# First mixture of experts on sorted 256-token tiles inside the attention batches

## What is computed

```
x  = x + tanh(g_xattn[0]) * attention0(layernorm(x), ctx)        # "att0": 16 heads of 8, 512 keys
x  = x + tanh(g_ffn[0])   * top1_mixture(layernorm(x))           # "m0": 8 experts, 128 -> 512 -> 128
x  = x + tanh(g_xattn[1]) * block(layernorm(x), ctx)             # "att1" self (256 keys), "att2" cross (512), "f" MLP
x  = x + tanh(g_ffn[1])   * layer(layernorm(x))                  # "att3" causal, "m1" 4 experts, top 2

def top1_mixture(x):                                             # x: 2048 tokens
    logits = x @ gate_w.T + gate_b
    top1 = argmax(logits, axis=-1)
    for e in range(8):
        h = relu(x @ w1[e].T + b1[e])
        y = h @ w2[e].T + b2[e]
        out = out + where(top1 == e, y, 0)
```

## Time and profile before

| | us |
|---|---|
| median of 3 runs | 1461.47 |
| lowest, highest | 1455.52, 1464.43 |
| the profiled execution | 1462.72 |
| its span, first to last instruction | 1460.9 |
| PE busy | 1272.8 |
| DVE busy | 861.5 |
| ACT busy | 692.7 |
| POOL busy | 306.1 |

### The profile page before, as it was taken

How to read it: one execution, slowest core, us unless ns; L and a number is a source line. 1 busy time by engine, 2 the same in 40 slices (tenths; PEclk the granted TensorE clock), 3 DMA queues, 4 the chain that set the end, 5 groups by cost and what they waited for, 6 DMA issues and landing times.

```text
span 1460.9 us, 25048 instructions
## 1 busy us (share of the span) xinstructions
PE 1272.8 (87%) x8296; PEld 664.8 (46%) x8296; DVE 861.5 (59%) x1890; ACT 692.7 (47%) x1064; POOL 306.1 (21%) x896
## 2 busy tenths in 40 slices
PE   3999899979999998788879998888888778879998
PEld 1444444534444443445434544444555556534333
DVE  2777767834443444577667776868665756533333
ACT  1466656633333432566646674554534334423333
POOL 3223222100001000233322231323232323100000
PEclk9999989989999999699979998998989879879999
DMA  7554544210001300455554453443324434220010
GB/s 187 162 154 143 147 128 131 74 48 8 15 22 38 104 3 22 131 165 167 156 177 128 145 148 102 133 124 111 106 78 131 120 99 138 63 55 21 22 29 15
DMA packets 163174, 144.32 MB, mean 99 GB/s; under 512 B 11739, under 2 KB 136931, under 8 KB 163043
## 3 DMA queue, kind: packets, MB, share of 16 engines
q1 hardware_dynamic: 163046, 142.72, 33.8%
HBM read 78.98 MB, written 62.91 MB: 97 GB/s over the span
## 4 chain that ended last, share of the span: by engine, by line
issue 65%; POOLq 22%; PE 10%; DVE 1%; DMA 1%; ACT 0%; DVEq 0%; POOL 0%; SPq 0%; PEldq 0%; ACTq 0%
POOLq L871 5%; POOLq L844 4%; PE e_ps L1580 3%; PE av_ps L1591 3%; PE e_ps L1581 3%; POOLq L841 2%; POOLq L846 2%; POOLq L879 2%; POOLq L881 2%; POOLq L883 2%; PE misc L1572 1%; POOLq L859 1%; POOLq L890 1%; POOLq L898 0%; PE misc L1360 0%
## 5 line engine op out<-in xcount | busy, mean ns | idle before, releaser
L930 ACT ACTIVATE prob<-e_ps 128x1024 f32<-128x1024 f32 (+1 forms) x384 | 378.2, 988 | 245.4 <-PE e_ps L1411 176.1
L1094 DVE TENSOR_REDUCE nmax<-s_ps 128x1 f32<-128x512 f32 x512 | 332.8, 685 | 116.3 <-PE s_ps L1374 114.1
L1411 PE MATMUL e_ps<-Qst,Kst 75*128 75x256 bf16 x1408 | 245.4, 288 | 19.4 <-DMA Qst<-mrow 12.1
L1374 PE MATMUL s_ps<-Kst,Qst 72*128 72x512 bf16 x512 | 208.9, 412 | 39.4 <-DVE nmax L1094 29.0
L1429 PE MATMUL av_ps<-prob,Vx 128*32 128x256 f32 (+1 forms) x3072 | 223.8, 411 | 0.8 <-ACT OT L935 0.8
L1411 PEld LDWEIGHTS e_ps<-Qst,Kst 75*128 75x128 bf16 x1408 | 139.8, 103 | 90.3 <-issue 24.4
L1218 DVE TENSOR_TENSOR prob<-prob,s_ps 128x512 f32<-128x512 f32 x128 | 87.8, 686 | 147.7 <-ACT prob L980 147.0
L980 ACT ACTIVATE prob<-e_ps,b 128x512 f32<-128x512 f32 x128 | 87.9, 687 | 147.5 <-PE e_ps L1510 146.9
L1510 PE MATMUL e_ps<-FB,wbig 128*128 128x512 f32 x256 | 137.4, 628 | 0.0
L1517 PE MATMUL av_ps<-prob,wbig 128*128 128x512 f32 x256 | 128.1, 592 | 0.0
L1429 PEld LDWEIGHTS av_ps<-prob,Vx 128*32 128x32 f32 x3072 | 92.8, 116 | 72.3 <-issue 38.9
(11 more groups left out here) (178 smaller groups left out, 1684.5 us busy)
## 6 DMA issues: line engine op xcount, KB each, us to landing
q_parts<-qp SPq DMA_DIRECT2D x96, 192.0 KB, 2.4
k_parts<-kp SPq DMA_DIRECT2D x48, 384.0 KB, 3.4
Qst<-q_parts SPq DMA_DIRECT2D x128, 144.0 KB
Kst<-k_parts SPq DMA_DIRECT2D x64, 288.0 KB
k_parts<-kp SPq DMA_DIRECT2D x48, 192.0 KB, 2.4
Kst<-k_parts SPq DMA_DIRECT2D x64, 144.0 KB
ctxT<-in_ctxT SPq DMA_DIRECT2D x16, 256.0 KB, 4.8
wbig<-in_w SPq DMA_DIRECT2D x16, 256.0 KB, 4.9
```

Of the source, the lines that this page charges most:

```text
L930: act.activation(dst, src, ACT.Exp).then_inc(e_drained, 1)
L1094: ve.tensor_reduce(nmax[:, g, u, h % GH:h % GH + 1], s_ps[:, c % 2, :], AX.X, ALU.max, negate=True).then_inc(s_drained, 1)
L1374: last = pe.matmul(s_ps[:, c % 2, :], Qst[0:ROWS, par, s, u * P:u * P + P], Ks[0:ROWS, par, s, :], start=True, stop=True)
L1411: last = pe.matmul(o, Ks[0:KROWS, par, h, t * P:t * P + P], Qst[0:KROWS, par, h, :], start=True, stop=not a.rope)
```

## The change

RUNS is one run of 32 batches. `moe0_steps` is gone, and att1 follows att0 directly. The mixture is done for each half of the batches (0 to 3, 4 to 7):

- Per batch of att0, two batches later or for the last of a half right behind it: gate logits from `nT`, the choice for 2 tiles of 128 tokens, and `m0.rank`: five small bfloat16 matmuls with a triangular and a ones matrix that count, for each token, the tokens of the same expert before it. The normalized rows stay in SBUF (`zg`) instead of going to DRAM transposed.
- `m0.plan` (three DVE steps per half): tiles of 256 tokens per expert, at most 4 + 7 = 11; the expert of each tile (`widx`), and the row of each token in the sorted order (`ypos`).
- `m0.scatter`, 8 per half: POOL scatters 128 rows of 512 B each by `ypos` to `xs_rows` in DRAM, which two transfers at the start have filled with zeros. `m0.wload`, 11 per half: POOL gathers the expert's weights, 128 rows of 1156 numbers (4.6 KB, 592 KB in all), into a ring of 4.
- For each tile: `m0.xload` (128 KB, SP), `m0.xT` (2 transposes, ACT copies), `m0.h` (4 matmuls of 256 columns into one buffer of `e_ps`, four relus), `m0.down` (8 matmuls with the tokens as stationary operand, 128 columns, into `misc`; DVE adds the bias), a store to `ys_rows`.
- Tiles of the first half begin in batch 5 at its middle, one per slot; those of the second in batch 9 (att1) at its middle, two per slot. A tile's three steps are in three successive slots.
- For each batch of att1: `loadx` loads the residual rows and POOL gathers twice 128 rows of `ys_rows`; DVE gates and adds, takes statistics, normalizes (`xapply`); PE transposes (`xT`); SP stores both (`xstore`). att1's `loadin` is gone.
- POOL: instead of `drain`, each operation adds to a semaphore and the next waits for it; each step waits for its own kind's last result.
- `body`: `weave` spreads the steps that use `misc` evenly over the score and AV units of the slot.

Weights of the second mixture and the MLP are loaded from batch 11 on. `prob`'s ring no longer counts the mixture (`RING_AT`). Cut to its core:

```
-RUNS = [(0, B), (B, N)]
+RUNS = [(0, N)]
...
+        per, rate = tile_pace(g)          # 16 // slots of the attention the tiles lie in, for both
+        put(n, TILES_AT - 2, ("m0.xload", g, 0), ("m0.xload", g, 1))
+        for k in range(NT):
+            p = TILES_AT + k // rate * per
+            if k + WRING < NT:
+                put(n, p + 3 * per, ("m0.wload", g, k + WRING))
+            if k + 2 < NT:
+                put(n, p + per, ("m0.xload", g, k + 2))
+        p = TILES_AT + (NT - 1) // rate * per + 2 * per + 2
+        m = B + HALF * g
+        put(n, p, ("loadx", m, None))
+        put(n, p + 1, ("loadx", m + 1, None))
+        put(n, p + 2, ("xstat", m, None))
+        put(n, p + 4, ("xapply", m, None))
+        put(n, p + 5, ("xT", m, None), ("xstore", m, None))
+        put(n, p + 6, ("q", m, None), ("qsplit", m, None), ("xstat", m + 1, None))
+        put(n, p + 7, ("k", m, None), ("ksplit", m, 0))
+        put(n, p + 8, ("qstore", m, None))
+        put(n, p + 9, ("kstore", m, None))
...
+        for x in range((NT - 1) // rate + 3):
+            for lag, kind in ((2, "m0.down"), (1, "m0.h"), (0, "m0.xT")):
+                tiles = range(rate * (x - lag), rate * (x - lag) + rate)
+                steps += [(kind, g, k) for k in tiles if 0 <= k < NT]
...
+        units[1:1] = [[st] for st in tiles if st[0] == "m0.h"]
+        out.append(("E", n, s))
+        out += weave(units, chunks)
...
+                elif kind == "m0.wload":
+                    po.wait_ge(m0_planned, 2 * n + 1)
+                    if arg >= WRING:
+                        wait_drained(po, ("m0.down", n, arg - WRING))
+                    elif n:
+                        wait_drained(po, ("m0.down", n - 1, NT - 1))
+                    index = bass.IndirectOffsetOnAxis(ap=widx[:, n, arg:arg + 1], axis=0)
+                    po.indirect_dma_start(out=w_0[:, arg % WRING, :], out_offset=None, in_=dram["w_0"], in_offset=index) \
+                        .then_inc(m0_win[arg % WRING], 16)
+                elif kind == "loadx" and n >= B:
+                    par, g = n % 2, (n - B) // HALF
+                    po.wait_ge(m0_ystored[0], 16 * Y_EVEN * (g + 1))
+                    po.wait_ge(m0_ystored[1], 16 * Y_ODD * (g + 1))
+                    po.wait_ge(x_stats, n - 1)
...
+                elif kind == "m0.h":
+                    c = SLOT[st]
+                    pe.wait_ge(m0_win[arg % WRING], 16 * (w_uses(n, arg) + 1))
+                    wait_drained(pe, ("m0.xT", n, arg))
+                    pe.wait_ge(e_drained, c - 1)
+                    for t in range(H0 // P):
+                        last = pe.matmul(e_ps[:, c % 2, t * TILE:(t + 1) * TILE], w_0[:, arg % WRING, t * P:t * P + P],
+                                         xs_T[:, arg % 2, :], start=True, stop=True)
...
+            for g in range(B // HALF):
+                blank = dram["blank"].unsqueeze(0).to_broadcast([NT, TILE, D])
+                sp.dma_start(xs_rows[g].rearrange("(n r) d -> n r d", r=TILE), blank).then_inc(blank_stored, 16)
...
-                po.drain()
-                po.tensor_copy(parts[:, 1, c0:c1], r[:, c0:c1])
-                po.drain()
+                settled()
+                counted(po.tensor_copy(parts[:, 1, c0:c1], r[:, c0:c1]))
+                settled()
```

More of the change, by code:

```diff
@@ L33 @@
 E0, H0 = 8, 512
+HALF = B // 2
+GT = HALF * QT
+TILE = 256
+NT = HALF * SQ // TILE + E0 - 1
+WRING = 4
+WCOLS = 2 * H0 + H0 // P + D
 E1, H1 = 4, 384
@@ L170, in ffn_items, with tile_pace, moe0_items, put @@
     return it
+def tile_pace(g):
+    per = 16 // att(HALF * g + HALF + TILES_AT // 16).slots
+    return per, per
+def moe0_items():
+    it = {}
+    def put(n, p, *steps):
+        it.setdefault((n + p // 16, p % 16), []).extend(steps)
+    for b in range(B):
+        if b % HALF < HALF - 1:
+            for p, kind in ((3, "m0.gate"), (6, "m0.choose"), (9, "m0.rank")):
+                put(b + 2, p, (kind, b, None))
+    for g in range(B // HALF):
+        last = HALF * g + HALF - 1
+        n = last + 1
+        for p, kind in ((11, "m0.gate"), (12, "m0.choose"), (13, "m0.rank")):
+            put(n, p, (kind, last, None))
+        for k in range(3):
+            put(n, 14 + k, ("m0.plan", g, k))
+        for k in range(WRING):
+            put(n, 16 + k // 2, ("m0.wload", g, k))
+        for j in range(GT):
+            put(n, 17 + j // 2, ("m0.scatter", g, j))
+        per, rate = tile_pace(g)
[17 more added lines that the diff above has]
+        put(n, p + 9, ("kstore", m, None))
+    return it
@@ new lines, in tile_items @@
+def tile_items():
+    it = {}
+    for g in range(B // HALF):
+        per, rate = tile_pace(g)
+        n = HALF * g + HALF
+        for x in range((NT - 1) // rate + 3):
+            steps = []
+            for lag, kind in ((2, "m0.down"), (1, "m0.h"), (0, "m0.xT")):
+                tiles = range(rate * (x - lag), rate * (x - lag) + rate)
+                steps += [(kind, g, k) for k in tiles if 0 <= k < NT]
+            p = TILES_AT + x * per
+            it[(n + p // 16, p % 16 // per)] = steps
+    return it
@@ L173, with opens_half @@
+def opens_half(n):
+    return B <= n < 2 * B and n % HALF == 0
 FFN_ITEMS = ffn_items()
+TILES_AT = 24
+MOE0_ITEMS = moe0_items()
+TILE_ITEMS = tile_items()
 QUARTERS = 4
@@ L424, in ring_users, with out_count @@
     return user
+RING_AT = count(("E", "f.h", "m1.h"))
 USER = ring_users()
-IN_PER = {"att0": 16, "att1": 16, "att2": 32, "att3": 16}
+IN_PER = {"att0": 16, "att1": 0, "att2": 32, "att3": 16}
+OUT_PER = {"att0": 16, "att1": 32, "att2": 32, "att3": 32}
 def in_count(n):
     return sum(IN_PER[att(m).name] for m in range(n % 2, n + 1, 2))
+def out_count(n):
+    return sum(OUT_PER[att(m).name] for m in range(n % 2, n + 1, 2))
 def program(nc, dram, outs):
```

666 lines of the change are left out of this document (348 added, 318 removed).

## The result

| | before | changed |
|---|---|---|
| median (lowest to highest) of the runs side by side | 1462.95 us (1455.52 to 1473.35, 4) | 1400.11 us (1397.82 to 1415.43, 4) |
| ratio, 95% interval | 1 | 0.959 (0.950 to 0.968) |
| profiled execution, span | 1462.72, 1460.9 us | 1398.62, 1396.8 us |
| mean granted TensorE clock | 0.927 | 0.896 |

The account below looks back on a forecast made before the run. The first mixture's stage was taken as bound by PE columns, 7 of 8 for experts not chosen. Terms: -273 + 42 + 42 + 20 + 8 + 10 + 5 + 12 + 8 - 12 = -138, giving 1325 us, range 1264 to 1400.

Parts of the forecast that it names:

- What was removed: Between att0 and att1: the first mixture's own stage and the two seams around it go, 273 us less.
- tiles: On PE: 22 added tiles at 3.83 us each lengthen their slots by their whole price, 42 us per half.
- rival B: Tile slots bound by their chains, PE at 1.2 GHz in them, tiles cost double: 1395 us, chance 0.18.
- Late weights: Second half's tiles 4 to 10 in att1 meet weights just asked for: four slots of 5 us, 20 us (4 to 40).
- Start-up: Two blanking transfers on SP's queue ahead of batch 0's q and k parts delay the first exponential: 10 us (0 to 20).
- The way into att1: Loading, gathering, normalizing and transposing att1's inputs: 1.5 us for each of 8 batches, 12 us (0 to 15).
- POOL's semaphores: On POOL: semaphores in place of drains change nothing, 0 us (-5 to +5).
- the new order of bank steps: Spreading the misc bank's steps over each slot saves some 1 us per batch over 32 batches: -12 us (-35 to +15).
- 0.4 to 1 us each, hidden, 0 on the path: 54 weight loads, scatters and gathers issued by POOL: hidden by POOL's slack, adding 0 us to the path.
- Rival C: Each of 54 indirect transfers holds POOL and the maxima's chain for 4.45 us: 1545 us, slower, chance 0.05.
- the choice: Choosing, ranking and planning on DVE in att0, mostly hidden in idle time: 0.6 us a batch, 5 us (0 to 23).

Follow-up runs that it names:

- e6: Changed kernel without the weight reloads for tiles 4 to 10 of each half, which use weights already in the ring: 1381.7 us, ratio 0.943.
- e14: e13 with the old order of slot steps in att1 batches without a tile (8 and 11 to 15) too: 1380.0 us, ratio 0.944.
- e13: e9 with the choice of each half's last batch also in five steps over three places, plan and transfers one place later: 1366.9 us, ratio 0.932.
- e2: Changed kernel with the old order of slot steps in the batches of att2 and att3 alone: 1377.3 us, ratio 0.940.
- e3: Kernel before with only the new order of slot units and bank steps: 1494.5 us, ratio 1.021.
- e8: Changed kernel with 2 of the 8 scatters per half, all tiles still computed: 1391.2 us, ratio 0.948.
- e12: Changed kernel without the weight reloads for tiles 4 to 10 and with only two of eight scatters per half: 1366.3 us, ratio 0.931.
- e9: Changed kernel with old order in att2 and att3, choice in five pieces except each half's last batch, and blanking stores issued later: 1361.5 us, ratio 0.935.
- e5: Changed kernel with the choice of batches 0-2 and 4-6 in five pieces at five places instead of one block: 1391.5 us, ratio 0.948.
- e4: Changed kernel with POOL ordered by drains again instead of semaphores: 1425.1 us, ratio 0.975.

## Why the prediction was wrong, point by point

What was removed was right: the stage and both seams went. The **tiles** were right where nothing else interferes: from the third slot with a tile (272.9 us) ten slots follow that take 5.5 to 6.3 us, 5.95 on average from exponential to exponential, at a granted clock of 1.00. So a tile adds 5.95 - 2.14 = 3.8 us (forecast 3.83). That also fells rival B, though its 1395 us is near the time: its cause, tile slots at 1.2 GHz, isn't there in att0, and the loss lies in other places. Only batch 9, at 0.75, has something of it.

**Late weights**: forecast 20, measured 18 at most (e6), though with three direct waits of 10.3 us in all and not four of 5. **Start-up**: forecast 10, measured 7.0. By the Trainium skill, DMA: Bandwidth & Descriptors, section on why a DMA increments its semaphore by 16, it would have been 14.5 (an estimate from that section's rule); the trace has half of that, so the rule's price did not show here. **The way into att1**: forecast 1.5 a batch; batches 11 to 15 take 124.2 us where they took 117.9, that is 1.3 each, but with 1.0 each that the new order saves there (e14 against e13), so the way in alone is nearer to 2.3. **POOL's semaphores**: 0 was right for the kernel before, but the question was put wrongly: what counts is not what they give before, but what the drains would cost beside the new transfers, 25 us.

Three steps failed.

First, **the new order of bank steps, "-12 (-35 to +15)"**. It was weighed by the direct waits for the bank and given to all 32 batches alike. Undone in att2 and att3 it gives 23 us back (e2), and alone it costs the kernel before 31 (e3), outside the range given. It is a small gain in att0 (2.6 us over seven batches, e3), a gain in att1 (7 to 13 us by e14) and a loss in att2, whose plain batches had run at 0.95 to 1.00, and in att3. Why the spread steps let it fall there, and not in att0, the runs don't say; that DVE's waits for the score matmul are longer in batch 17 with it (8.2 us, 4.5 in e2) only names the place. In the table of stretches this step is 36 us of the error: 24 in att2 and att3, and 12 that were counted as a gain. Counted net it is less: 23 lost, 3 and 7 to 13 gained, so 7 to 13 lost in all for 12 forecast as gained. The term was off by 19 to 25, and the gain in att0 and att1 covers 10 to 16 us of what else went wrong there.

Second, **"I take 0.4 to 1 us each, hidden, 0 on the path"** for the 54 transfers on POOL. The size was right (about 1 us, and 0.30 behind it), the cover wasn't. They don't come singly: ten, with the splits of q and k among them, stand before one split of a maximum, 8.4 us of waiting PE. POOL's share of busy time, a third, says nothing about such a row. Sending fewer gives 9 us (e8) to 15 (e12 against e6). Rival C had this mechanism, with a price of 4.45 us for each where POOL was held 1.0, and 1.3 with the gap behind it; and it counted every transfer as exposed.

Third, **the choice, "0.6 us a batch"**. DVE's free 8 us per batch were there, and still did not hide a block of six operations that stands ahead of a maximum. Batches 2 to 4 are 14 us over their forecast; put in pieces the choice costs 1.4 a batch (e9), and 9 us come back in all (e5). The sum of the operations was right (the six take 1.4 us); what was not seen is that the block makes TensorE wait and that stretches at 1.2 GHz come with it, 10.2 us long in batch 3.

The clock runs through all three. Its mean fell from 0.927 to 0.896. A share of 1 - 0.896 of 1396.8 us is 145 us, against 107 of 1460.9 before. Counted over TensorE's busy time alone, the changed kernel loses some 36 us more by its clock. This is no fourth cause: it is a part of what the three cost. The prediction, which worked out each term from rows at either level, had outside rival B no term for work that changes its level. In e9 the mean is 0.918.

Of the 74 us of error (1398.6 less 1324.7), 19 to 25 are the order counted net, 9 to 15 POOL's row, 14 the choice, less 3 at the start. The remaining 23 to 35 stay open. About half of it is in batches 5 and 6, 15 us over forecast: PE waits 3.46 us for the first sorted rows, and the second part of batch 6, with batch 8's way in, runs at 0.81. Some 3 of it went with the choice in pieces (e5, batch 6: 55.5 us for 58.6); no run took the rest out alone. What else the change moved (the loads of the second mixture's weights, the tail of the batches that end a half) was not tried by itself either.

## What to carry to other kernels

Price a step that is put ahead of a full engine's input by the longest unbroken block it makes on its own engine, not by its share of that engine's free time; and price a wait of TensorE with the stretch at 1.2 GHz that may follow it. An order that helps one stage (a lower clock before, a full one after) may spoil another: try it stage by stage, look at each stage's granted clock, and keep it only where that rises. Before moving transfers to POOL, list what stands in one row on its queue, and what waits behind the row's end.

## What the runs showed of the hardware that was not expected

- An indirect transfer held POOL for 0.94 to 1.04 us in 52 of 54 cases (1.18 and 1.21 in the others), whatever it moved (64 KB of rows or 592 KB of weights), mostly with 0.30 us to the next one in a row; a drain behind it lasted 3.5 to 7.8 us.
- 592 KB of weights by index land 5.7 us after the start of their issue (median of the 12 of 22 whose landing the trace gives, 4.2 to 6.6); 256 KB on SP's queue before took 4.9. By the Trainium skill, DMA: Bandwidth & Descriptors, section on the anatomy of one DMA on the gpsimd path, 592 KB would take 2.0 + 592 / 436 = 3.4 us (an estimate from its fit); the trace has 2.3 more.
- A short wait of TensorE (1.46 us) in a stream that is otherwise full was followed by 10.2 us at a granted clock of 0.50, during which it is 98% busy. It is no rule: a wait of 1.45 us at 136.7 us was followed by none for 13 us, and in batch 17 a fall comes 1.3 us after a wait of 1.14.
- Between dependent operations of POOL a semaphore takes less than a drain: 0.28 us from start to start of an operation of 0.20 in the changed kernel (436.82 to 437.10), 0.34 with drains (448.71 to 449.05 in e4). In the kernel before this moved nothing.
